# A four-batch transformer block: third norm of the last half on VectorE, expert tiles re-dealt, fills in the steady batch

## What is computed

```python
def _ripple(x, Wqkv, Wo, conv_w):          # 8 heads of 16 channels
    q, k, v = jnp.split(x @ Wqkv, 3, axis=-1)
    # offsets 0, 1, 2, 4 ... 512: each token attends to 11 earlier ones
    w = softmax(q . k[pos - offsets] / sqrt(16))
    tele = sum(w * v[pos - offsets])
    conv = depthwise causal convolution of v, 7 taps
    low = (fq @ (fk^T v)) / (fq . sum(fk) + 1e-06)     # fq, fk = elu + 1
    return (tele + conv + low) @ Wo
def _ffn(x):
    scores = sigmoid(x @ gate_W) * route_scale         # 8 experts, best 2, weights normalised
    expert_out = sum over experts of gate * (gelu(x @ W1 + b1) @ W2 + b2)
    return expert_out + gelu(x @ Ws1 + bs1) @ Ws2 + bs2
x = x + layernorm(x_n + _ripple(x_n)),  x_n = layernorm(x)     # norms 1 and 2
x = x + layernorm(_ffn(layernorm(x)))                          # norms 3 and 4
```

## Time and profile before

| | |
|---|---|
| runs | 297.0, 302.2, 296.45 us; median 297.0 |
| profiled execution | 296.57 us |
| its span, first to last instruction | 294.7 us |
| busy in the span | PE 248.8 (84%), DVE 231.7 (79%), ACT 198.2 (67%), POOL 94.7 (32%) |
| mean granted clock of TensorE | 0.959 of full speed |

### The profile page before, as it was taken

The page is one execution under the profiler, slowest core; times in us unless marked ns, Lnnn a source line. Parts: engine busy times, 40 slices in busy tenths (PEclk is TensorE's granted clock), DMA queues, the critical chain, the costliest instruction groups (busy, mean ns, idle before and its releaser), DMA issues.

```text
span 294.7 us, 4732 instructions
## 1 busy us (share of the span) xinstructions
PE 248.8 (84%) x1593; PEld 173.7 (59%) x1593; DVE 231.7 (79%) x598; ACT 198.2 (67%) x461; POOL 94.7 (32%) x152
## 2 busy tenths in 40 slices
PE   5857978886989699979988699979969699899893
PEld 5413774884625377858625377758526578774383
DVE  6699798489997848889889757999589699627653
ACT  2475465637969768849977777939876747476841
POOL 5920161028272124044562024053531131430023
PEclk9997997999899799989999799979999999999999
DMA  7437989300689943500899934201799863000003
GB/s 197 110 97 233 225 190 201 75 0 2 181 232 191 233 83 71 146 0 4 241 230 223 183 77 93 53 1 33 241 215 225 191 122 73 1 1 2 0 14 95
DMA packets 24258, 35.27 MB, mean 120 GB/s; under 512 B 4053, under 2 KB 17198, under 8 KB 24234
## 3 DMA queue, kind: packets, MB, share of 16 engines
q1 hardware_dynamic: 20346, 21.59, 25.7%
q0 software_dynamic: 3888, 13.37, 25.3%
HBM read 5.07 MB, written 2.10 MB: 24 GB/s over the span
## 4 chain that ended last, share of the span: by engine, by line
PE 47%; DVE 22%; ACT 18%; POOL 7%; issue 4%; DMA 1%; POOLq 0%; DVEq 0%; ACTq 0%
DVE prods L282 10%; PE psH L1365 7%; PE psF L1424 7%; PE psA L1271 6%; PE psY L1462 6%; POOL rstd L483 4%; PE psA L1462 3%; PE psA L1333 2%; ACT xn L597 2%; DVE x L1068 2%; POOL var L481 2%; PE psG L1462 2%; PE psA L1263 1%; PE psG L1448 1%; ACT L691 1%
## 5 line engine op out<-in xcount | busy, mean ns | idle before, releaser
L282 DVE TENSOR_TENSOR prods<-qT,kT 128x1024 f32<-128x1024 f32 (+1 forms) x48 | 50.7, 1112 | 7.2 <-PE psA L1333 5.0
L483 POOL TENSOR_TENSOR rstd<-var,neg_half 128x4 f32<-128x4 f32 (+2 forms) x28 | 41.2, 1472 | 2.3
L1365 PE MATMUL psH<-ident,prods 128*128 128x128 f32 x324 | 39.9, 273 | 0.0
L481 POOL TENSOR_SCALAR var<-ss 128x4 f32<-128x4 f32 (+1 forms) x25 | 10.2, 407 | 91.6 <-ACT squares L765 35.3
L1365 PEld LDWEIGHTS psH<-ident,prods 128*128 128x128 f32 x324 | 36.4, 141 | 2.3 <-issue 2.3
L1037 DVE TENSOR_TENSOR prods<-v_shift,prob 128x896 f32<-128x896 f32 x32 | 34.7, 1085 | 0.0
L1424 PE MATMUL psF<-x3T,w 128*128 128x512 f32 x58 | 29.0, 611 | 1.0 <-ACT hid L741 0.6
L1333 PE MATMUL psA<-prods,slot_sel 128*32 128x512 f32 x168 | 24.3, 627 | 3.7 <-DVE prods L282 2.4
L1271 PE MATMUL psA<-xnT,wqkv 128*128 128x512 f32 x36 | 22.1, 752 | 5.5 <-ACT xnT L586 5.5
L1150 DVE TENSOR_TENSOR hid<-hid,psG 128x512 f32<-128x512 f32 x32 | 20.8, 683 | 6.3 <-PE psG L1448 5.7
L741 ACT ACTIVATE hid<-psF,b1c 128x512 f32<-128x512 f32 x29 | 19.1, 688 | 8.8 <-PE psF L1424 8.7
(11 more groups left out here) (241 smaller groups left out, 583.5 us busy)
## 6 DMA issues: line engine op xcount, KB each, us to landing
v_shift<-v_tok SPq DMA_DIRECT2D x20, 448.0 KB
convT<-tapT POOLq DMA_DIRECT2D x8, 512.0 KB, 5.7
x_res<-L_attn_x SPq DMA_DIRECT2D x4, 512.0 KB, 10.0
tapT<-tapT POOLq DMA_DIRECT2D x4, 512.0 KB, 10.9
out<-y_out SPq DMA_DIRECT2D x7, 256.0 KB, 3.9
x_in<-L_attn_x SPq DMA_DIRECT2D x3, 512.0 KB, 4.9
v_shift<-v_tok SPq DMA_DIRECT2D x4, 384.0 KB
convT<-kexp POOLq DMA_DIRECT2D x3, 512.0 KB, 10.3
```

The lines of the kernel that those rows point to most:

```text
L282: return eng.tensor_tensor(prods[:, QUADS * (s % 2) + q, t0:t1], qT[:, t0:t1], kT[:, PRE - off + t0:PRE - off + t1], ALU.mult)
L481: nc.gpsimd.tensor_scalar(var[:, cols], src, scale, EPS, ALU.mult, ALU.add).then_inc(step, 1)
L483: return nc.gpsimd.tensor_tensor(rstd[:, cols], var[:, cols], neg_half[:, cols], ALU.pow)
L1365: ins = pe.matmul(dst, terms[:, j % TERM_BUFS, m, :], ident[:], is_transpose=True, start=False, stop=(m == live[-1]))
```

## The change

The diff, cut to its parts:

```diff
-FILL_LAST = 10
+FILL_LAST, FILL_K, FILL_OUT = 12, 18, 14
...
+        def spread_bank(u, c):
+            return psF[:, 3 - c, :] if u == 2 * B - 1 and c >= 2 else psG[:, c % 2, :]
...
+            def last_ln3():
+                pool.wait_ge(last_var, 1)
+                nc.gpsimd.tensor_tensor(rstd3[:, TPH:NT], var3[:, TPH:NT], neg_half[:, TPH:NT],
+                                        ALU.pow).then_inc(last_rstd, 1)
...
                         gate_logits(u0)
-                        scale_taps(b, range(4, 6))
+                        scale_taps(b, range(4, TAPS))
...
+            def last_variance():
+                u, tiles = 2 * B - 1, slice(TPH, NT)
+                dve.wait_ge(ss2_ready, u + 1)
+                dve.wait_ge(x_res_ld, upto(u // 2, N_DMA, N_DMA))
...
+                for n, j in enumerate(range(TPH, NT)):
+                    ins = nc.vector.scalar_tensor_tensor(out=scratch[:, n, :], in0=attended(1)[:, bass.ts(n, P)],
+                                                         scalar=2.0 / P, in1=x_res[:, j, :], op0=ALU.mult, op1=ALU.mult,
+                                                         accum_out=cross[:, n:n + 1])
+                last_chain(ins)
+                dve.wait_ge(ln2_ready, u + 1)
+                last_chain(nc.vector.scalar_tensor_tensor(out=var3[:, tiles], in0=ss2[:, tiles], scalar=1.0 / P,
+                                                          in1=rstd2[:, tiles], op0=ALU.mult, op1=ALU.mult))
+                last_chain(nc.vector.tensor_tensor(var3[:, tiles], var3[:, tiles], cross[:], ALU.add))
+                last_chain(nc.vector.tensor_tensor(var3[:, tiles], var3[:, tiles], rstd2[:, tiles], ALU.mult))
+                nc.vector.scalar_tensor_tensor(out=var3[:, tiles], in0=var3[:, tiles], scalar=EPS,
+                                               in1=mv[:, tiles, 1], op0=ALU.add, op1=ALU.add).then_inc(last_var, 1)
...
+            def last_normalise():
+                dve.wait_ge(last_rstd, 1)
+                for j in range(TPH, NT):
+                    last = nc.vector.tensor_scalar(xn3[:, j, :], x2_of(u)[:, j, :], neg_mean[:, u // 2 % 3, j:j + 1],
+                                                   rstd3[:, j:j + 1], ALU.add, ALU.mult)
...
-                    residual(2 * b)
+                    if not more:
+                        residual(2 * b)
                     add_conv(b, 1)
+                    if more:
+                        residual(2 * b)
+                    else:
+                        gate_hidden(u1, range(2, 4))
...
                         turn_logits(u0)
+                        if b >= 2:
+                            experts_out(u0 - 1, range(TPH - 1, TPH))
...
                     turn_scores(b)
+                    low(b)
                     if ffn:
                         gates_expert_major(u0)
-                    low(b)
...
+                    if more and ffn:
+                        pe.wait_ge(hidden_free, upto(u1, N_HIDDEN, -1))
+                        keep_busy(FILL_K, front(u1, X3))
                     if more:
                         project_k(b + 1)
...
+                    if more:
+                        if ffn:
+                            pe.wait_ge(gated, upto(u1, 4, 4))
+                        keep_busy(FILL_OUT, psG[:, 1, :])
+                    else:
+                        spread_gates(u1, range(2, 4))
                     output(b, 1)
```

More of the change, by code:

```diff
@@ L814, in _ @@
                         evacuate_x3(u1)
-                        scale_taps(b, range(6, TAPS))
                         evacuate_shared(u1)
@@ L1213, in _ @@
                         if ffn:
-                            if j in (6, 7):
+                            if j == 6 or j == 7 and more:
                                 gate_hidden(u1, range(2 * (j - 6), 2 * (j - 5)))
@@ L1230, in _ @@
                     gates(u1, range(done, N_GATE_STEPS))
+                    finish(u0 - 1)
                     gate_hidden(u1, range(0, 4))
-                    finish(u0 - 1)
                     finish(u0)
@@ L1445, in spread_gates @@
                         pe.wait_ge(gT_ready, u + 1)
-                    if c >= 2 or u == 2 * B - 1:
+                    if u == 2 * B - 1 and c >= 2:
+                        pe.wait_ge(hidden_free, upto(u, N_HIDDEN, 2 * c - 2))
+                    elif c >= 2 or u == 2 * B - 1:
                         pe.wait_ge(gated, upto(u, 4, c - 1))
-                    pe.matmul(psG[:, c % 2, :], gate_sel[:, c, :], gT[:, u % 2, :], start=True, stop=True).then_inc(gate_spread, 1)
+                    pe.matmul(spread_bank(u, c), gate_sel[:, c, :], gT[:, u % 2, :], start=True, stop=True).then_inc(gate_spread, 1)
             def experts_out(u, tiles=range(TPH)):
@@ L1537, in _ @@
                                 gates_expert_major(u1)
-                            if j in (5, 7):
+                            if j == 5 or j == 7 and more:
                                 spread_gates(u1, range(j - 5, j - 3))
@@ L1555, in _ @@
                         gate_logits(2 * b)
-                    if ffn:
-                        experts_out(u1, range(TPH - 1, TPH) if more else range(TPH - 1))
+                    elif ffn:
+                        experts_out(u1, range(0, 2))
                 else:
@@ L1570, in _ @@
                     turn_logits(u1)
-                    hidden(u0, range(2, 4))
+                    hidden(u0, range(1, 3))
                     gates_expert_major(u0)
+                    hidden(u0, (3,))
                     spread_gates(u0, range(0, 2))
```

52 lines of the change are left out of this document (31 added, 21 removed).

## The result

The changed kernel takes 289.2 us (median of four runs, 287.68 to 289.54), the kernel before 297.3 beside it. The ratio is 0.9727 with a 95% interval of 0.9678 to 0.9776: 8.1 us faster, where 10.1 were forecast. The ratios leave out executions that ran some per cent longer at a lower clock, like the one of 302.2 us of the kernel before, while the medians keep them. The profiled execution took 289.32 us, its span 287.3 (before 296.57 and 294.7).

What follows compares the result with a forecast made beforehand. The kernel was taken as a relay between TensorE, VectorE and ScalarE; terms +0.7 - 1.5 + 0.5 - 2.9 - 0.5 - 2.2 - 4.2 = -10.1 took 296.57 to 286.5 us, range 283.5 to 292.0.

Steps and rivals of the forecast that it cites:

- Part 1: Seam of batches 0 and 1: convolution added before the residual must wait for TensorE's last sum; 0.7 us slower.
- Part 2: Batch 1: 18 fill passes ahead of the keys hold the clock, keys 1.72 us for 3.07; 1.5 us faster.
- Parts 3 and 4: Seam of batches 1 and 2: +0.5 us, later gate exponential; batch 2: low-rank term before gates, key fill, -2.9 us.
- Parts 5 and 6: Seam of batches 2 and 3: score sums sooner, -0.5 us; batch 3: shorter waits for hidden chunks, -2.2 us.
- Part 7: Last half: earlier last output, third norm from sums at hand, gates sooner, shorter TensorE end; 4.2 us faster.
- The fills don't hold the clock: Rival: key projections of batches 1 and 2 lose 1.5 + 1.6 us of gain, giving 289.6 us; chance 0.13.
- The last half gains only its first step: Rival: only the 1.2 us at the last output stays, 3 us less gain, giving 289.5 us; chance 0.08.
- Slower: Rival: the half-rate clock falls in TensorE's dense stretches; 17 us of work so caught give 303.5 us; chance 0.06.
- Both seams paid in full: Rival: GpSimd blocked at each seam plus one loss in fills or last half, giving 292.2 us; chance 0.13.

## Why the prediction was right, and where it was short

The direction, the places and most sizes were right; the gain was 2.0 us short by the medians and 2.8 us by the traces (7.3 us between the two profiled times). Of the 2.8 the last half is 1.2, batches 1 and 3 are 0.4 each, and 0.9 is the variation of single executions in batch 0. The runs that undo or add one part give, by their ratios, 2.5 for the fills ahead of the keys, 4.8 for the order of gates and low-rank term, 1.9 for the last half and -1.0 for the residual in batch 0, 8.2 in sum, beside the measured 8.1; each is uncertain by a microsecond or more.

*Part 1, +0.7:* measured +0.64 in the traces, 0.9 by the medians with the run that undoes it. Right.

*Part 2, the fill in batch 1.* Forecast -1.5; up to the key features of batch 2 it was -1.1. The keys started 33.65 us behind the key features for 33.09, since ScalarE's normalised x came later. GpSimd in the kernel before, then GpSimd and VectorE in the changed kernel, at the seam of batches 0 and 1:

```profile
79.29 1.08 POOL L496 TENSOR_SCALAR neg_mean<-mv 128x8 f32<-128x8 f32 x1 [6.60 <-DVE mv L924]
80.44 1.07 POOL L481 TENSOR_SCALAR var<-mv 128x8 f32<-128x8 f32 x1
```

```profile
80.63 2.33 DVE L286 TENSOR_TENSOR prods<-qT,kT 128x1024 f32<-128x1024 f32 x2
80.81 3.44 POOL L504 TENSOR_SCALAR neg_mean<-mv 128x8 f32<-128x8 f32 x1 [6.60 <-DVE mv L935]
82.96 1.22 DVE L286 TENSOR_TENSOR prods<-qT,kT 128x1024 f32<-128x1024 f32 x1
84.59 1.64 POOL L491 TENSOR_TENSOR rstd<-var,neg_half 128x8 f32<-128x8 f32 x1
```

An operation that took 0.20 us at the next seam of the kernel before takes 3.44 and ends at 84.25, where the third product ends (84.18). In the second trace of the changed kernel it took 1.08 and the power 2.57, and the chain was 0.55 us shorter; there the stretch is 35.20 us and the sum -1.7. The kernel before has 1.08, 1.07 and 2.57 as well, at the same distance behind the key features, and so have all of the other traces. So the collision at this seam was there already, the change didn't bring it, and the fill's step was right; what took 0.55 us is a rarer form of it that stands in this one trace of fourteen. The Trainium skill ("SBUF — State Buffer", Who interferes with whom) has a VectorE instruction with two SBUF inputs contend with GpSimd's reads; the rows beside the products (1.08 to 3.44 us for 0.20) agree.

*Parts 3 and 4, batch 2.* Forecast -2.4 together, measured -2.13 and -0.36. The steps in detail, VectorE, GpSimd and ScalarE at the seam:

```profile
145.65 1.64 POOL L491 TENSOR_TENSOR rstd<-var,neg_half 128x8 f32<-128x8 f32 x1
146.30 0.21 ACT L746 ACTIVATE gexp<-psF 128x32 f32<-128x32 f32 x1
146.54 0.18 DVE L1132 TENSOR_SCALAR gtmp<-gexp 128x32 f32<-128x32 f32 x1 [1.04 <-ACT gexp L746]
149.35 1.13 DVE L1201 SCALAR_TENSOR_TENSOR y_out<-psG,rstd,x 128x128 f32<-128x128 f32 x4 [0.67 <-POOL rstd L491]
```

The exponential comes 1.04 us later behind the key features, as said, VectorE's wait for the score sums is now one for it, and the finish starts 0.2 us later, for 0.5. Only the power didn't stretch (1.64 for 2.5): VectorE waited just then, and the two small operations ahead of it took 1.08 and 1.07 us instead. The new order of gates and low-rank term was undervalued (4.8 us by the run that undoes it, for 1.3 + 2.2), the fill ahead of the keys overvalued as a sure 1.6: 1.28 us in an execution with a spell, nothing in one without. That the sum fits is luck in part, since two wrong sizes cancel, and it rests on one execution of each kernel. Two readings of mine were off besides: by its own rows the fill ahead of the keys was worth 168.03 - 166.55 = 1.5 us, not 1.6, and VectorE without its wait reaches the gate step at 144.30 - 1.41 + 2.37 = 145.3, not 144.9.

*Parts 5 and 6, batch 3.* Forecast -2.7, measured -2.29. The step that fell short is ScalarE's wait for hidden chunks, 0.83 us where I left 0.3; and the expert tile costs 0.9 us here, by the run with it put back, which I had booked as "most of it back".

*Part 7, the last half.* Forecast -4.2, measured -0.96 - 2.03 = -3.0; 0.24 of the miss are ahead of the last output (0.96 for 1.2). Five of its times were met within 0.6 us, counted from the last output: x3 ready at 7.3 us (6.9 forecast), turned at 9.0 (8.6), the even half's gates begun at 8.8 (8.3), the last half's at 14.4 (13.8), done at 21.7 (21.3). The last gate exponential came at 12.6 for 11.8, but VectorE was not yet there. That x3 would be ready before TensorE comes, and 12.7 us from the last turn of x3 to the last gates, held to the digit. The term that was mis-sized was the seam to TensorE's end: 10.43 us for 9.9. I let TensorE be at the gates when they are done; its expert tile holds it until 273.09, 0.85 us after them. The other half of the miss is the even half's small turn, which waits 0.4 us behind an expert tile (257.38 above). Neither is work, both are order.

*The rivals.* "The fills don't hold the clock" is refuted by the 2.0 us of the run without those ahead of the keys. "The last half gains only its first step" is refuted by 32.15 us for 34.19 behind the last output with only that part changed. "Slower": in the page's forty slices the changed kernel's clock is at 9 tenths or more from 79 us to the slice before the last; its low slices stand near 24 us and behind the waits of 3.19 and 2.87 us, in batch 0 and the front of batch 1. "Both seams paid in full": the first seam cost 0.64 us for the 1.4 of that rival, the second 0.2 at the finish for 2.

## What to carry to other kernels

Price a fill as a chance, not as a sum: what it saves is the spell times how often that wait is followed by one, and the surer edit is the one that takes the wait away, because it takes the spell along. Before moving work off a chain, write down which engine has no gap from the first to the last step of the stretch (here VectorE for 12.98 us) and look for what stands ahead of the one instruction that it starts with. And an edit applied to all batches may pay in one and cost in another: look at each, since two edits, each undone in one batch, together took 1.6 us off the stretches of the trace (1.1 by the ratio, within its interval).

## What the runs showed of the hardware that I had not expected

*The same wait is followed by a low spell in one execution and not in the next.* I took every wait of TensorE of 1.8 us or more, from 45 us on, in all fourteen traces, and the mean granted clock over the 3 us behind it; under 0.8 counts as low:

| wait | times | low behind it |
|---|---|---|
| 1.82 to 1.87 us | 14 | 1 |
| 1.97 to 2.44 us | 17 | 10 |
| 2.70 to 2.87 us | 14 | 9 |
| 3.18 to 3.35 us | 14 | 13 |

The kernel before had ten waits over 1.3 us and six low spells behind them, the changed kernel four and two. The low share grows with the wait's length, but length and place can't be told apart here: 13 of the last row's waits are one place, in batch 0, and the only one elsewhere (3.35 us, in batch 1 of the run without output fills) had no spell; ten of the first row are one place in batch 3. Nor does each spell cost time: behind the 2.87 us wait ahead of the turn of v in batch 1, which seven traces have, three had one, and the two of these with the usual GpSimd chain took 35.19 us from the key features to the turn of x3, for 35.20 without a spell. A spell costs where TensorE is the engine waited for, as in the run without key fills (1.28 and 1.66 us). The Trainium skill ("TensorE: Matmul & The Clock Gate", What's actually happening) says that the gate's judgement is not tied to the kernel's start, so that the place where the clock changes differs between runs; the 2.87 us wait agrees, the same place in seven traces with a spell in three, and so do the two waits of 2.75 us in the run without key fills.

*GpSimd gets in between VectorE's products, not beside them.* A 0.20 us operation ended with the first product in one execution of the changed kernel (1.08 us) and with the third in the other (3.44 us), from the same start relative to them, within 0.01 us. In all fourteen traces the longer form stands once; why it came then isn't shown.
